# Count matrices of a graph kernel: strips of 16 destinations instead of 25, one 480-column matmul per chunk, four rotating PSUM banks, two chunks per run

## The reference, cut to what matters

```python
dst = jnp.minimum((1250 * jax.random.uniform(..., (40000,)) ** 2.0).astype(jnp.int32), 9999)
_o = jnp.argsort(dst, stable=True)
...
denom = jax.ops.segment_sum(ee, dst, num_segments=n)          # attention
...
onehot = jax.nn.one_hot(edge_type, NUM_REL, dtype=h.dtype)    # convolutions
count = jax.ops.segment_sum(onehot, dst, num_segments=num_nodes)
msg = msg * inv[dst, edge_type][:, None]
agg = jax.ops.segment_sum(msg, dst, num_segments=num_nodes)
```

## Time and profile before

| what | value |
|---|---|
| median of 3 runs | 2808.84 us (2806.64 to 2812.04) |
| span of the profiled execution | 2808.8 us |
| the loop over windows | from 45.6 to about 401 us of the span |
| in it: PE busy, DVE busy | 321.6 and 255.0 us |
| next stage's first transfer | at 427.9 us |

### The profile page before, as it was taken

One profiled execution on the slowest core, in us unless ns is written; L12 is line 12 of the kernel. 1 busy time (PEld: TensorE's weight loads), 2 busy tenths in 40 slices (PEclk: granted clock), 3 DMA queues, 4 the chain that ended last, 5 costly groups with the idle time before them and its releaser, 6 DMA issues.

```text
span 2808.8 us, 36704 instructions
## 1 busy us (share of the span) xinstructions
PE 2302.6 (82%) x13674; PEld 2042.3 (73%) x13675; DVE 1309.6 (47%) x1838; ACT 525.6 (19%) x994; POOL 251.4 (9%) x137
## 2 busy tenths in 40 slices
PE   3988860002788887999999999999999999999996
PEld 3988860000333336899898999999999999999996
DVE  7876744799999995421211214311212133121233
ACT  0122220001455553110101102200101022010100
POOL 0011210043110000000000000010000000101000
PEclk9999885555999998999999999999999999999998
DMA  0133333101101003221221201221212111313131
GB/s 15 44 76 80 86 83 114 67 28 54 37 36 52 37 18 99 69 73 54 61 59 39 74 12 41 69 68 37 80 46 64 37 35 60 84 42 83 54 95 60
DMA packets 103671, 162.98 MB, mean 58 GB/s; under 512 B 68847, under 2 KB 68950, under 8 KB 103511
## 3 DMA queue, kind: packets, MB, share of 16 engines
q1 hardware_dynamic: 66000, 100.11, 11.8%
q0 software_dynamic: 37520, 60.59, 8.0%
HBM read 129.53 MB, written 30.66 MB: 57 GB/s over the span
## 4 chain that ended last, share of the span: by engine, by line
PE 56%; DMA 2%; DVE 2%; issue 1%; ACT 0%; DVEq 0%; SPq 0%
PE pp L976 30%; PE pa L946 26%; DMA back<-s_x 1%; DMA out_dram<-back 1%; DVE norm_stats L1073 0%; PE pp L956 0%; DVE acc L1069 0%; DMA w_raw<-in_L_gnn_w_root_dram 0%; DVE g_lo L1156 0%; DVE back L1085 0%; DVE w_lo L1145 0%; DVE acc L1121 0%; DVE back L1069 0%; DVE h_lo L1104 0%; DVE h_lo L1108 0%
## 5 line engine op out<-in xcount | busy, mean ns | idle before, releaser
L946 PE MATMUL pa<-ct_in,h_hi 125*128 125x250 f32 x2850 | 705.4, 287 | 34.0 <-issue 34.0
L946 PE MATMUL pa<-ct_in,h_lo 125*128 125x250 f32 x2850 | 702.8, 285 | 0.0
L1156 DVE TENSOR_TENSOR g_lo<-pa,g_hi 128x250 fp32r<-128x250 f32 x400 | 166.7, 417 | 1110.0 <-ACT g_hi L1050 1109.7
L946 PEld LDWEIGHTS pa<-ct_in,h_hi 125*128 125x128 f32 x2850 | 556.5, 195 | 43.5 <-issue 42.3
L946 PEld LDWEIGHTS pa<-ct_in,h_lo 125*128 125x128 f32 x2850 | 558.9, 196 | 0.9
L976 PE MATMUL pp<-w_hi,g_hi 128*125 128x384 f32 (+2 forms) x1600 | 434.8, 353 | 8.6 <-DVE g_lo L1156 8.5
L976 PE MATMUL pp<-w_lo,g_hi 128*125 128x384 f32 (+2 forms) x1600 | 430.2, 350 | 0.0
L1050 ACT CAST g_hi<-pa 128x250 fp32r<-128x250 f32 x400 | 147.1, 368 | 1437.4 <-PE pa L946 1437.4
L976 PE MATMUL pp<-w_hi,g_lo 128*125 128x384 f32 (+1 forms) x1520 | 405.4, 348 | 0.0
L796 PE MATMUL po<-pw,xh 125*65 125x418 f32 x720 | 283.3, 533 | 79.1 <-DVE pw L733 78.3
L976 PEld LDWEIGHTS pp<-w_lo,g_hi 128*125 128x125 f32 (+1 forms) x1600 | 294.6, 187 | 11.1
(11 more groups left out here) (154 smaller groups left out, 1209.8 us busy)
## 6 DMA issues: line engine op xcount, KB each, us to landing
ct_in<-s_ct POOLq DMA_DIRECT2D x45, 1220.7 KB, 16.8
s_ct<-ct_stage SPq DMA_DIRECT2D x30, 610.4 KB
w_raw<-in_L_gnn_w_rel_dram SPq DMA_DIRECT2D x39, 384.0 KB, 3.1
uv<-s_uv SPq DMA_DIRECT2D x24, 610.4 KB
w_raw<-in_L_gnn_w_rel_dram SPq DMA_DIRECT2D x21, 448.0 KB, 3.3
uv<-s_scores SPq DMA_DIRECT2D x12, 610.4 KB
w_raw<-in_L_gnn_w_root_dram SPq DMA_DIRECT2D x13, 384.0 KB, 3.1
x_tile<-in_x_dram SPq DMA_DIRECT2D x10, 375.0 KB
```

What stands on the lines that cost most here:

```text
L946: ins = nc.tensor.matmul(pa[0:rows, n % 2, 0:GP], a, b, start=i == 0, stop=i == len(pairs) - 1)
L1156: nc.vector.tensor_tensor(g_lo[0:rows, n % 3], pa[0:rows, n % 2, 0:GP], g_hi[0:rows, n % 3].bitcast(F32), ALU.subtract).then_inc(lo_done, 1)
```

## The change

Windows become WD = 16 destinations wide. Each tile of 125 destinations is numbered as if it had PAD = 128, so that eight windows make a tile (the last one with 13 real destinations) and there are 80 windows. For that DVE computes a padded destination `dtile` ahead of the keys (four more operations). A key has 480 columns, so a chunk is one matmul of 480 columns into one bank, and the four banks of `win` rotate with the window. `oh_rem` and `zero_a` get 128 columns (126 before). A run is CG = 2 chunks, and `oh_key` is still `[CH, 2, CG, ...]`. ACT evacuates a window with one copy. The range of a window is packed with 8 bits instead of 7. The scores move from window 3 to window 4 of a tile. `edges_more` only takes room.

```diff
-CG = 4
+CG = 2
-WD = 25
-NW = N // WD
-WT = T // WD
+WD = 16
+PAD = 128
+WT = PAD // WD
+NW = NT * WT
...
         oh_key = sb("oh_key", [CH, 2, CG, NT * KEY], BF16)
...
-        oh_rem = sb("oh_rem", [CH, T + 1, NCH], BF16)
-        zero = sb("zero_a", [CH, T + 1], BF16)
+        oh_rem = sb("oh_rem", [CH, PAD, NCH], BF16)
+        zero = sb("zero_a", [CH, PAD], BF16)
...
-        win = ps("win", [T + 1, 2, 2, 512], F32)
+        win = ps("win", [PAD, WB, 512], F32)
...
+            nc.vector.tensor_scalar(dtile[:], flt[:, 1], float((1 - T) / 2), 1.0 / T, ALU.add, ALU.mult).then_inc(padded, 1)
...
+            nc.vector.tensor_scalar(dtile[:], dtile[:], MAGIC, None, ALU.add).then_inc(padded, 1)
...
+            nc.vector.tensor_scalar(dtile[:], dtile[:], -MAGIC, None, ALU.add).then_inc(padded, 1)
...
+            nc.vector.scalar_tensor_tensor(out=dtile[:], in0=dtile[:], scalar=float(PAD - T), in1=flt[:, 1],
+                                           op0=ALU.mult, op1=ALU.add).then_inc(padded, 1)
...
-                    act.wait_ge(win_full[w % 2], tt * WT + w // 2 + 1)
-                    for m in range(2):
-                        nc.scalar.copy(
-                            stage[:, b, :, m * BANK:(m + 1) * BANK, i * WD:(i + 1) * WD],
-                            win[:, w % 2, m, 0:BANK * KEY].rearrange("p (s r d) -> p r s d", s=BANK, r=R)
-                        ).then_inc(evac[w % 2], 1)
+                    act.wait_ge(win_full[w % WB], tt * (2 * WT // WB) + w // WB + 1)
+                    d = min(WD, T - i * WD)
+                    nc.scalar.copy(
+                        stage[:, b, :, :, i * WD:i * WD + d],
+                        win[0:T + 1, w % WB, 0:NT * KEY].rearrange("p (s r d) -> p r s d", s=NT, r=R)[:, :, :, 0:d]
+                    ).then_inc(evac[w % WB], 1)
...
                     for b in range(CG):
                         pe.wait_ge(oh_ready[p][b], n + 1)
-                        for m in range(2):
-                            ins = nc.tensor.matmul(win[:, p, m, 0:BANK * KEY], oh_rem[:, :, bass.ds(q * CG + b, 1)].rearrange("e s c -> e (s c)"),
-                                                   oh_key[:, p, b, m * BANK * KEY:(m + 1) * BANK * KEY],
-                                                   start=False, stop=False, skip_group_check=True)
-                        ins.then_inc(oh_used[p][b], 1)
+                        nc.tensor.matmul(win[:, w % WB, 0:NT * KEY], oh_rem[:, :, bass.ds(q * CG + b, 1)].rearrange("e s c -> e (s c)"),
+                                         oh_key[:, p, b], start=False, stop=False,
+                                         skip_group_check=True).then_inc(oh_used[p][b], 1)
```

More of the change, by code:

```diff
@@ L117, in count_matrices @@
         oh_used = [[sem(f"oh_used{p}{b}") for b in range(CG)] for p in range(2)]
-        win_full = [sem(f"win_full{b}") for b in range(2)]
-        evac = [sem(f"evac{b}") for b in range(2)]
+        win_full = [sem(f"win_full{b}") for b in range(WB)]
+        evac = [sem(f"evac{b}") for b in range(WB)]
         stored = [sem(f"stored{b}") for b in range(2)]
         half = sem("csum_half"); summed = sem("summed"); turned_c = sem("turned_c"); tp_free = sem("tp_free")
-        magic = sem("magic"); csum_kept = sem("csum_kept")
+        magic = sem("magic"); padded = sem("padded"); csum_kept = sem("csum_kept")
         w_in = sem("w_in"); cleared = sem("cleared"); small_turned = sem("small_turned")
@@ L128, in tile_staged @@
         def tile_staged(eng, tt, b):
-            eng.wait_ge(evac[0], (tt * WT + (3, WT)[b]) * 2)
-            eng.wait_ge(evac[1], (tt * WT + (2, WT)[b]) * 2)
+            for m in range(WB):
+                eng.wait_ge(evac[m], (tt * 2 + b + 1) * (WT // WB))
         def run_range(eng, w):
-            both = nc.s_assert_within(eng.value_load(tab[0:1, bass.ds(w, 1)]), 0, NRUN * 128 + NRUN,
+            both = nc.s_assert_within(eng.value_load(tab[0:1, bass.ds(w, 1)]), 0, NRUN * 256 + NRUN,
                                       skip_runtime_bounds_check_because=WITHIN)
-            return (nc.s_assert_within(eng.snap(both >> 7), 0, NRUN - 1, skip_runtime_bounds_check_because=WITHIN),
-                    nc.s_assert_within(eng.snap(both & 127), 1, NRUN, skip_runtime_bounds_check_because=WITHIN))
+            return (nc.s_assert_within(eng.snap(both >> 8), 0, NRUN - 1, skip_runtime_bounds_check_because=WITHIN),
+                    nc.s_assert_within(eng.snap(both & 255), 1, NRUN, skip_runtime_bounds_check_because=WITHIN))
         block = ctx.enter_context(nc.Block())
@@ L229, in _ @@
             dve.wait_ge(magic, 4)
-            nc.vector.scalar_tensor_tensor(out=key[:], in0=key[:], scalar=float(N), in1=flt[:, 1],
+            dve.wait_ge(padded, 4)
+            nc.vector.scalar_tensor_tensor(out=key[:], in0=key[:], scalar=float(NT * PAD), in1=dtile[:],
                                            op0=ALU.mult, op1=ALU.add).then_inc(keyed, 1)
-            nc.vector.tensor_reduce(ends[:, 0], flt[:, 1], AX.X, ALU.min).then_inc(ends_ready, 1)
-            nc.vector.tensor_reduce(ends[:, 1], flt[:, 1], AX.X, ALU.max).then_inc(ends_ready, 1)
+            nc.vector.tensor_reduce(ends[:, 0], dtile[:], AX.X, ALU.min).then_inc(ends_ready, 1)
+            nc.vector.tensor_reduce(ends[:, 1], dtile[:], AX.X, ALU.max).then_inc(ends_ready, 1)
             dve.wait_ge(small_turned, 1)
@@ L318, in _ @@
         def _(act):
-            act.wait_ge(consts, 9)
+            act.wait_ge(consts, 10)
             def keep_turned(g):
@@ L395, in _, with zeros_onto @@
                 pe.reg_mov(items[p], 0)
-            def zeros_onto(p, m, start):
-                return nc.tensor.matmul(win[:, p, m, 0:1], zero[:], zero[:, 0:1], start=start, stop=False,
+            def zeros_onto(m, start):
+                return nc.tensor.matmul(win[:, m, 0:1], zero[:], zero[:, 0:1], start=start, stop=False,
                                         skip_group_check=True)
```

31 lines of the change are left out of this document (18 added, 13 removed).

## The result

| | before | change |
|---|---|---|
| time, median of 4 runs (us) | 2807.7 (2806.6 to 2812.0) | 2922.2 (2919.8 to 2924.8) |
| profiled execution: span (us) | 2808.8 | 2923.1 |
| one-hot matrices, matmuls on them | 516, 1032 | 476, 476 |
| start of first, of last one-hot matrix (us) | 45.62, 395.90 | 47.95, 514.9 |

The change is slower: ratio 1.0404, interval 1.0392 to 1.0417, so +114 us. The forecast was 2877 with 2822 to 2912: the sign was right, the size 45 us short, and the time lies 10 us above the range.

What follows compares the result with a forecast made beforehand. Two oh_key buffers' round trip was to bind, with the clock mostly low. Loop 313 + 22 + 36 + 48 = 419 against 352.5 (+66.5), +2.4 ahead, -0.3 for ACT: +69, so 2877 us, range 2822 to 2912.

Steps and rivals of the forecast that it cites:

- The trip T: Loop over windows: a two-buffer round trip takes 1.315 us (1.365 low clock, 1.165 high); 238 runs give 313 us.
- The clock's fall behind a thin stretch: Loop: sparse PE matmuls drop the granted clock, so three quarters of the loop runs at the low level.
- PE's other work: Per-tile PE work in the loop: 10 us, four stops each hiding about 1.3; 4.8 a tile, 48 us by ten.
- Change of window: Border between windows in the loop: each adds 0.27 us to a trip, 22 us over 80 windows.
- POOL: One-hot matrices beside POOL's additions in the loop: 18 stalls costing 2.0 us each, 36 us.
- Ahead of the loop: Before the loop: four more DVE operations, 2.0 us, and wider range arithmetic, about 0.4; 2.4 us together.
- What would show it: Profile after: pairs 1.2 to 1.45 us apart, some 400 DVE waits over 150 us, PE idle likewise, clock near 0.5.
- 1: Loop: the high clock stays, with the long load; T 1.25 us, 2836 us in all; chance 0.13.
- 3: Loop: short load and high clock, so no measurable change; 2800 to 2815 us; chance 0.08.
- 4: Window borders: runs overlap there with middle load and high clock, so faster; 2793 us; chance 0.06.
- Rival 2: Loop: low clock throughout and the long load; T 1.45 us, 2907 us in all; chance 0.11.
- the middle load: Weight load in each trip: taken midway between no change and -0.17 us, so 0.085 us shorter.

Runs made afterwards that it cites:

- e1_ring4: The changed kernel with a second slot for every oh_key buffer, chosen by the parity of the run's number: 2819.3 us, ratio 1.0040.
- e9: The kernel before with 128 weight columns, runs of two chunks and two slots for each oh_key buffer: 2817.1 us, ratio 1.0030.
- e4: The kernel before with 128 weight columns instead of 126, the two more being zeros: 2787.2 us, ratio 0.9926.
- e12: The changed kernel with 126 weight columns instead of 128: 2951.9 us, ratio 1.0508.
- e3: The kernel before with runs of two chunks instead of four, so two oh_key buffers to a parity: 2912.2 us, ratio 1.0371.
- e2: The changed kernel with runs of four chunks instead of two, so four oh_key buffers to a parity: 2806.4 us, ratio 0.9992.
- e5_filler: The changed kernel with one more 480-column matmul of zero weights behind each chunk's matmul: 2858.8 us, ratio 1.0182.
- e6_change_few_pieces: The changed kernel with only two of six residual slices and one of six score slices computed: 2869.3 us, ratio 1.0217.
- e10_half_width: The changed kernel with one-hot matrices of only the first 240 of 480 columns: 2909.3 us in a single run.

## Why the prediction was right in sign and short in size

- **Two buffers set the pace by their round trip**: shown by e1_ring4, which changes only the slots and gives back 103 us. Runs of four give back 116 and halving the run in before costs 105, but both also change the number of loop steps; e9 against e4 puts about 30 us on halved runs where the ring is deep.
- **Narrow windows are not free**, and my sum had them only in the count of runs and changes of window: they cost 39 us with two buffers (e12 against e3), 19 with runs of four (e2 against e4) and 3 with runs of two and a deep ring (e1 against e9), and in the change the short load takes 30 back. What of it is more runs, more windows or the four banks was not separated.
- **The trip T** was put at 1.315, and the first class has 1.34 on average, 238 x 0.02 = 5 us more. (The table counts from 1.374, which makes it 14 more here and 3 less in the first class.) The clock in it was right: I took a quarter of the trips at the high clock, and 17 of 74 were short. At the low clock I had 1.365 and it is 1.374, at the high one 1.165 and 1.18. That is luck in part, for two errors nearly cancel. The load came out 0.17, near its lower bound and not at the middle: e12_change_126 shows it at 0.12 a trip where I took off 0.085 (-0.035). And the one-hot matrix did not shrink with its columns: 0.40 instead of 0.48 - 0.14 = 0.34 (+0.06).
- **The clock's fall behind a thin stretch**, which the forecast took over to the new rhythm. These stretches of before follow the nine matmuls in 3.4 us of the earlier trace rows (columns as above):

```profile
110.80:114.20 3.40, 1.49 (x4) 1.01 (x5) 3.40 (x4) 0.00 (x0) 2.29 (x1) 0.50 0.37 83
114.20:117.60 3.40, 3.40 (x12) 3.40 (x12) 2.65 (x6) 0.00 (x0) 0.00 (x0) 0.51 0.38 83
117.60:121.00 3.40, 3.39 (x21) 3.29 (x21) 2.51 (x6) 1.28 (x3) 0.00 (x0) 1.00 0.38 82
```

  Four matmuls, then twelve on a PE that is busy throughout, at 0.50 and 0.51, then 21 at 1.00. The clock's records have nine such stretches in the loop of before, of 3.4 or 6.8 us at 0.50, and each begins 1.8 to 5.7 us behind the start of POOL's first addition. In the change 0.50 is the usual level and 1.00 comes for 3.4 us at a time, once for 6.8: 0.60 over 76.8 to 517.2 us. That the thin rhythm causes it is shown by e5_filler alone, where PE gets 476 matmuls more and the clock is 0.93. How thin a stretch must be no run shows.
- **The failed step: PE's other work.** I took 10 us a tile and 1.3 hidden at each of four stops, 48 in all; the gaps show 90. Two errors, about equal. (a) I took it partly at the high clock, and nearly all of it ran at the low one (104 of the residual's 110 gaps between neighbouring matmuls are about 0.21 us, where the filler's are 0.11), as the clock rose only behind it (0.50 over 165.6 to 175.8 us, which holds the scores of the rows below to their end at 175.1, and 1.00 over 175.8 to 179.2): 12 us a tile, 2 x 10 = 20 us more. (b) A stop hides less than a whole trip. I let the pair that DVE has ahead cover T; but that pair has only been made when the work ends, and its load, its matmul and the way back to DVE are still to come. The scores show it:

```profile
168.89 1.05 PE L426 MATMUL win<-oh_key,oh_rem 125*128 125x480 bf16 x2 [0.33 <-DVE oh_key L317]
...
169.81 2.69 PE L451 MATMUL scores<-u,xT_tile 128*125 128x24 f32 x12
169.81 0.72 DVE L317 TENSOR_SCALAR oh_key<-iota_key,edge_cols,minus_window 125x480 bf16<-125x480 uint16 x2 [0.69 <-issue]
...
172.43 2.70 PE L453 MATMUL scores<-xT_tile,u 128*24 128x125 f32 x12
...
175.91 0.72 DVE L317 TENSOR_SCALAR oh_key<-iota_key,edge_cols,minus_window 125x480 bf16<-125x480 uint16 x2 [5.38 <-PE win L426]
```

The work lasts 172.43 + 2.70 - 169.81 = 5.3 us, DVE's gap is 175.91 - 169.81 = 6.1, so 6.1 - 1.37 = 4.7 fall on the loop and 0.6 are hidden: the time of one matrix and the way to PE. On average it is 12 - 90/10 = 3.0 a tile, 0.75 a stop. e5_filler shows (a) together with what it does to the trip (this work falls from 119 to 69 us, the gaps behind it by 55), e6_change_few_pieces that cutting 58 us of this work saves 53; that (b) is the start of the trip and not another wait is read from the rows and was not tried by itself.
- **Change of window**: 22 predicted, 12 + 11 = 23 in the gaps. **POOL**: 36 predicted, 30. **Ahead of the loop**: 2.4 predicted, 47.95 - 45.62 = 2.3. The first and the last are right within what such terms can be, POOL's is 6 too high.
- **The sum**: 327 + 20 + 90 + 30 = 467 (the -3 with the 23) against 419. The last transposes of the summed counts start 523.77 - 407.26 = 116.5 us later than in the earlier trace rows; the stages behind them take 2 us less, which I did not follow up.
- **What would show it**: pairs 1.2 to 1.45 apart, the first window (19 runs in 26.2 us), the clock near 0.5 to 0.6 in slices 2 to 7, the short load and DVE's waits over 150 us all came. Three signs were wrong. PE idle for DVE was to be over 150 us like DVE's wait for PE; it is 95. I said one-hot matrices 0.25 apart within a pair; they are about 0.32 to 0.38 apart. And I said 400 waits; it is 159, about one for each of the 238 runs but the 80 that begin a window, since the second matrix of a pair is free by the time the first is made.
- **Rivals**: 1, 3 and 4 needed the high clock and fell with it (0.60 in the loop). Rival 2 had the clock nearly right and the load wrong; its 2907 is nearest only because the long load stood in for the work of PE that I had priced too low. The forecast itself owes some of its nearness to the middle load: with the load that came (0.035 less a trip) and nothing else mended it would have been 8 us lower.

## What to carry to other kernels

Count a ring in time, not in buffers: the number of buffers times the producer's step should reach one full round trip (here 2 x 0.32 to 0.38 us against 1.18 to 1.37), and a diff that halves the length of a run may halve the ring with it. In these rows work that the consuming engine does in between was hidden only up to the point at which the first waiting item could have been taken (0.6 of 5.3 us), and it grew from 6.7 to 12 us a tile when the granted clock went from 0.92 to 0.60 in the thinner rhythm. Padding the strided weights from 126 to 128 columns took their load from 0.31 to 0.17 us, which saved 20 us of this kernel, and costs two columns of zeros. Shorter runs lost each time they were tried, with fewer chunks to do: 105 us (e3 against before), 30 (e9 against e4), 13 (e1 against e2); with a deep ring the rows show a fixed cost of a run on both engines (e1_ring4: 0.24 us on DVE, 0.35 on PE). And when a variant equals the reference, look for two effects that cancel: here the padding hid the price of narrow windows.

## What the runs showed of the hardware that I had not expected

- **A granted clock of 1.00 can mean that there is no record.** Three stretches of the changed kernel (columns as above):

```profile
60.00:74.00 14.00, 10.71 (x22) 3.52 (x22) 7.82 (x20) 0.00 (x0) 0.00 (x0) 1.00 0.00 0
77.00:80.00 3.00, 2.15 (x6) 0.85 (x5) 1.67 (x6) 0.00 (x0) 0.00 (x0) 1.00 0.30 103
...
87.00:95.00 8.00, 6.12 (x13) 2.08 (x13) 4.33 (x12) 0.55 (x1) 0.00 (x0) 0.50 0.00 0
```

  The trip is 1.37 in the first (60.34 to 61.71), 1.18 in the second (77.44 to 78.62) and 1.38 in the third (89.55 to 90.93). The first record of the clock in this trace begins at 76.8 us, and everything ahead of it reads 1.00; its trips have the length of the low clock. From the record on, trips and clock agree: of the 74 plain trips the 17 of 1.18 or 1.19 have their first matmul where the record says 1.00, or less than 0.15 us ahead of it, and none of the others there has. Each trace has its own start: 49.3 us in before, 54.7 in e5_filler, 90.8 in e3_before_cg2, so the 1.80 of that run's pairs at 60 us is the low clock as well.
- **More matmuls made the kernel faster**: 476 of no use took off 63 us, with the loop's granted clock at 0.93 instead of 0.60 (both from the first record on).
- **A one-hot matrix of 240, 480 or 750 columns takes 0.34, 0.40 and 0.48 us** (e10_half_width, the change, before): by the line through these three, an estimate, some 0.28 of each doesn't depend on the columns.
